# Pairing the tiles of the plain layer norms: one logarithm and one exponential for two tiles' variances, and six banks for centered tiles

## The reference

```python
def _layernorm(x, axis=-1, eps=1e-05):
    m = jnp.mean(x, axis=axis, keepdims=True)
    v = jnp.var(x, axis=axis, keepdims=True)
    return (x - m) / jnp.sqrt(v + eps)

def _ln(x, g, b, eps=1e-05):
    mu = jnp.mean(x, axis=-1, keepdims=True)
    var = jnp.var(x, axis=-1, keepdims=True)
    return (x - mu) * jax.lax.rsqrt(var + eps) * g + b
```

## Time and profile before

| | us |
|---|---|
| runs | 3423.56, 3425.92, 3431.12; median 3425.92 |
| the profiled execution: its own time | 3423.85 |
| its span, first to last instruction | 3422.1 |
| busy: PE, DVE, ACT, POOL | 3107.2, 2148.8, 1799.2, 1170.2 |
| one norm of the gamma kind, from its first matmul to its last DVE operation | 20.5 |

### The profile page before, as it was taken

The page is one execution under the profiler, slowest core; times in us unless marked ns, Lnnn a source line. Parts: engine busy times, 40 slices in busy tenths (PEclk is TensorE's granted clock), DMA queues, the critical chain, the costliest instruction groups (busy, mean ns, idle before and its releaser), DMA issues. The chain is left out here.

```text
span 3422.1 us, 62042 instructions
## 1 busy us (share of the span) xinstructions
PE 3107.2 (91%) x22950; PEld 1935.5 (57%) x22971; DVE 2148.8 (63%) x4177; ACT 1799.2 (53%) x3979; POOL 1170.2 (34%) x1166
## 2 busy tenths in 40 slices
PE   7999989999999999998898879997699999998999
PEld 6999866446464646446654543334366566664444
DVE  7999744025353545337847744445699999974777
ACT  1232245564746474755644433334466666664666
POOL 4666511001010101105626612224477777760000
PEclk9999989999999999999999989998899999999999
DMA  2000000000000000000000022220100000003676
GB/s 86 20 15 10 1 19 12 1 7 1 6 1 6 1 6 4 3 7 1 1 8 1 1 64 56 57 51 16 24 11 5 4 5 4 5 1 45 72 68 65
DMA packets 75395, 66.43 MB, mean 19 GB/s; under 512 B 20374, under 2 KB 70584, under 8 KB 74680
## 3 DMA queue, kind: packets, MB, share of 16 engines
q1 hardware_dynamic: 75096, 62.45, 10.7%
HBM read 55.58 MB, written 2.51 MB: 17 GB/s over the span
## 5 line engine op out<-in xcount | busy, mean ns | idle before, releaser
L707 ACT ACTIVATE p_hidden<-p_hid_ps,net_bias 128x344 f32<-128x344 f32 x816 | 381.9, 548 | 229.2 <-PE p_hid_ps L654 170.0
L2447 POOL TENSOR_TENSOR p_qt<-p_qt,p_q_sum 97x512 f32<-97x512 f32 (+1 forms) x44 | 46.3, 1053 | 734.2 <-DVE p_q_sum L2401 734.2
L680 PE MATMUL p_y_ps<-p_hidden,net_down 128*64 128x344 f32 x1632 | 284.6, 468 | 4.2 <-DVE p_hidden L756 4.1
L654 PE MATMUL p_hid_ps<-xn,net_up 64*128 64x344 f32 x1248 | 241.6, 488 | 8.2 <-PEq L316 4.6
L2759 DVE TENSOR_TENSOR p_hid<-p_silu,p_pair_ps 128x344 f32<-128x344 f32 x288 | 134.8, 509 | 173.1 <-PE p_pair_ps L2708 95.1
L756 DVE TENSOR_TENSOR p_hidden<-p_hidden,p_row 128x344 f32<-128x344 f32 x384 | 175.6, 515 | 74.4 <-ACT p_hidden L707 47.0
L2740 ACT ACTIVATE p_silu<-p_pair_ps 128x344 f32<-128x344 f32 x288 | 116.0, 455 | 201.6 <-PE p_pair_ps L2697 201.6
L1919 POOL TENSOR_TENSOR p_rot<-p_rot,p_cross 128x512 f32<-128x512 f32 x128 | 160.4, 1274 | 127.3 <-DVE p_cross L2074 127.3
L680 PEld LDWEIGHTS p_y_ps<-p_hidden,net_down 128*64 128x64 f32 x1632 | 102.8, 136 | 158.9 <-issue 49.2
L1932 POOL TENSOR_TENSOR p_prob<-p_prob,p_total 128x1024 f32<-128x1024 f32 (+1 forms) x128 | 185.4, 1469 | 13.1 <-DVE p_total L2100 13.1
L654 PEld LDWEIGHTS p_hid_ps<-xn,net_up 64*128 64x128 f32 x1248 | 105.9, 189 | 129.0 <-ACT p_hidden L707 78.7
(11 more groups left out here) (465 smaller groups left out, 8102.6 us busy)
## 6 DMA issues: line engine op xcount, KB each, us to landing
p_row<-gated_rows SPq DMA_DIRECT2D x192, 86.0 KB, 2.9
p_row<-mark_rows SPq DMA_DIRECT2D x192, 86.0 KB, 10.3
tok_x<-in_tok_x SPq DMA_DIRECT2D x11, 384.0 KB, 3.1
out<-h SPq DMA_DIRECT2D x12, 172.0 KB, 3.7
shared_value_pairs<-shared_values SPq DMA_DIRECT2D x16, 128.0 KB, 2.5
p_swapped<-xn SPq DMA_DIRECT2D x64, 32.0 KB, 1.9
p_x<-in_tok_x SPq DMA_DIRECT2D x5, 384.0 KB, 3.1
p_kinds<-in_tok_c3w SPq DMA_DIRECT2D x1, 1280.0 KB, 7.2
```

The costliest lines, as they stand in the source:

```text
L654: mm = pe.matmul(hid_ps[k % ring][:, 0:TILE], w_up[half(g), n, :], x[half(g), cols(t)], start=True, stop=not experts or by_rows)
L680: mm = pe.matmul(y_ps[u][half(g), 0:TILE], w_down[:, n, :], hid[k % hidden_ring][:], start=n == 0, stop=last and not experts)
L707: act.activation(hid[k % hidden_ring][:], hid_ps[k % ring][:, 0:TILE], func, bias=b_up[:, n:n + 1]).then_inc(act_done.sem, 1)
```

## The change

Tiles are taken in pairs. `var_ps` becomes one tensor of two banks, with an even tile's variances in the first and an odd tile's in the second; `both` is a view of 2 x 344 columns over them. One logarithm and one exponential of 688 columns (`roots(n)`) take the place of two each of 344. The four banks of `var_ps` become two, and the four of `centered_ps` six. `square` has four buffers, `rstd` three of two tiles each. `variance(t)` of an even tile now waits until the logarithm of the pair before has read the two banks, and stands two places behind `spread` in PE's order in place of one. ACT does the two squares of a pair, then logarithm and exponential of the pair before. DVE's order stays, with each `scale` waiting for its pair's exponential.

```diff
-    nc, banks, ring = tower.nc, 4, 3
+    nc, banks, ring, turns = tower.nc, 6, 4, TILES // 2
...
-        var_ps = [ph.ps(f"var{r}") for r in range(banks)]
+        var_ps = ph.ps("var", (P, 2 * BANK))
         square = [ph.sb(f"square{r}", [P, TILE]) for r in range(ring)]
-        rstd = [ph.sb(f"rstd{r}", [P, TILE]) for r in range(ring)]
+        rstd = [ph.sb(f"rstd{r}", [P, 2, TILE]) for r in range(3)]
+        both = var_ps[:].rearrange("p (i c) -> p i c", c=BANK)[:, :, 0:TILE]
...
                     pe.wait_ge(squared.sem, squared.at(t + 1))
-                    if t >= banks:
-                        pe.wait_ge(logged.sem, logged.at(t - banks + 1))
-                    pe.matmul(var_ps[t % banks][:, 0:TILE], tower.average[:], square[t % ring][:],
+                    if t >= 2 and t % 2 == 0:
+                        pe.wait_ge(logged.sem, logged.at(t // 2))
+                    pe.matmul(both[:, t % 2, :], tower.average[:], square[t % ring][:],
                               start=True, stop=True).then_inc(var_ready.sem, 1)
-                for s in range(TILES + 1):
+                for s in range(TILES + 2):
                     if center and s < TILES:
                         spread(s)
-                    if s >= 1:
-                        variance(s - 1)
+                    if s >= 2:
+                        variance(s - 2)
...
+                def roots(n):
+                    act.wait_ge(var_ready.sem, var_ready.at(2 * n + 2))
+                    if n >= 3:
+                        act.wait_ge(scaled.sem, scaled.at(2 * (n - 2)))
+                    act.activation(rstd[n % 3][:], both, ACT.Ln, bias=tower.eps[eps]).then_inc(logged.sem, 1)
+                    act.wait_ge(logged.sem, logged.at(n + 1))
+                    act.activation(rstd[n % 3][:], rstd[n % 3][:], ACT.Exp, scale=-0.5).then_inc(rooted.sem, 1)
+
+                for n in range(turns + 1):
+                    if n < turns:
+                        squares(2 * n)
+                        squares(2 * n + 1)
+                    if n >= 1:
+                        roots(n - 1)
...
-                    dve.wait_ge(rooted.sem, rooted.at(t + 1))
+                    dve.wait_ge(rooted.sem, rooted.at(t // 2 + 1))
```

More of the change, by code:

```diff
@@ L116, in norm_phase @@
 def norm_phase(tower, src, dst, eps, center=True, gamma=None, beta=None, clip=None, residual=False, pos=None, loads=(), then=None):
-    nc, banks, ring = tower.nc, 4, 3
+    nc, banks, ring, turns = tower.nc, 6, 4, TILES // 2
     with phase(tower) as ph:
         centered_ps = [ph.ps(f"centered{r}") for r in range(banks)]
-        var_ps = [ph.ps(f"var{r}") for r in range(banks)]
+        var_ps = ph.ps("var", (P, 2 * BANK))
         square = [ph.sb(f"square{r}", [P, TILE]) for r in range(ring)]
-        rstd = [ph.sb(f"rstd{r}", [P, TILE]) for r in range(ring)]
+        rstd = [ph.sb(f"rstd{r}", [P, 2, TILE]) for r in range(3)]
+        both = var_ps[:].rearrange("p (i c) -> p i c", c=BANK)[:, :, 0:TILE]
         centered = ph.counts(TILES if center else 0)
-        squared, var_ready, logged, rooted, scaled = [ph.counts(TILES) for _ in range(5)]
+        squared, var_ready, scaled = [ph.counts(TILES) for _ in range(3)]
+        logged, rooted = ph.counts(turns), ph.counts(turns)
         loaded = ph.counts(16 * len(loads))
@@ L198, in scale @@
                 def scale(t):
-                    dve.wait_ge(rooted.sem, rooted.at(t + 1))
+                    dve.wait_ge(rooted.sem, rooted.at(t // 2 + 1))
                     if gamma is None:
-                        ins = dve.tensor_tensor(dst[:, cols(t)], values(t), rstd[t % ring][:], ALU.mult)
+                        ins = dve.tensor_tensor(dst[:, cols(t)], values(t), rstd[t // 2 % 3][:, t % 2, :], ALU.mult)
                     else:
-                        ins = dve.scalar_tensor_tensor(dst[:, cols(t)], values(t), gamma, rstd[t % ring][:],
+                        ins = dve.scalar_tensor_tensor(dst[:, cols(t)], values(t), gamma, rstd[t // 2 % 3][:, t % 2, :],
                                                        ALU.mult, ALU.mult)
```

## The result

| | before | changed |
|---|---|---|
| median of 5 runs, us | 3425.73 (3423.56 to 3431.12) | 3441.69 (3437.97 to 3445.26) |
| profiled execution / span, us | 3423.85 / 3422.1 | 3437.97 / 3436.2 |
| ratio changed / before | | 1.0045, 95% interval 1.003 to 1.006 |
| a gamma norm at full clock, us | 20.54 | 21.77 |
| busy ACT, us | 1799.2 | 1778.2 |

The change made the kernel 16.0 us slower (3441.69 - 3425.73). ACT did 21.0 us less work and nothing came of it.

What follows compares the result with a forecast made beforehand. Neither PE nor ACT was full; waits around four centered banks bound each norm. The new waits added +12.1 us over 15 norms, giving 3436.0 from the profiled execution and 3438.0 from the median; middle 3437, range 3427 to 3448.

Steps and rivals of the forecast that it cites:

- The ring: In each norm, logarithm end to logarithm end: hand-over 0.05, variance matmul 0.68, spread 0.58, second variance 0.77, logarithm 0.82; 2.90 us a pair.
- the tail: End of a gamma norm after the last exponential: five DVE operations, 2.04 us, against 1.23 before.
- The exposed weight load: A matmul that had to wait loads its weights in the open: next matmul 0.68 us later, against 0.58 in a stream.
- the hand-over from ACT to PE: From a logarithm's end to the start of the variance matmul waiting for it: 0.05 us, an estimate.
- the kinds: Norm calls by type: gamma 8 (+6.6 us), two-tensor 3 (+3.3), one-step 2 (+1.2), clip 1 (+0.9), uncentered 1 (-0.7).
- the sum: All 15 norms together: 6.6 + 3.3 + 1.2 + 0.9 - 0.7 + 0.8 = +12.1 us.
- cold starts: Two norm calls that begin at half clock, with one more matmul before their first logarithm: 0.4 us each, +0.8.
- The uncentered norm: The one call without spreads: 2.32 us between logarithms, 15.8 us against 16.5 before, -0.7.
- one of the two things that by the forecast would show it wrong: Forecast wrong if logarithms stood under 2.75 us apart, or if the uncentered call weren't the only one to become shorter.
- The third rival: TensorE idle 1.4 us after a norm's dummy matmuls, against 0.92, drops the clock at half the norms: +17, 3454; chance 0.09.
- The first rival: Reordering lets weight loads run ahead, so 0.58 replaces 0.68: 9 us less over all norms, 3429; chance 0.15.
- The second: Rival: waiting for the logarithm isn't last; PE's matmuls (2.32) or ACT's work (up to 2.50) pace a pair: 3410; chance 0.06.

Runs made afterwards that it cites:

- the kernel with PE's order in pairs: Changed kernel with TensorE doing both spreads of a pair, then both variances of the pair before: 3448.14 us, ratio 1.0066 to before; gamma norm 19.88 us.

## Why the prediction was right, and where it was off

The forecast was 3437 (range 3427 to 3448), slower, with 0.77. The time is 3441.69.

The ring was right in its members and its place, and the kernel with PE's order in pairs shows that it sets the pace. Forecast 2.90 us, measured 2.99. The logarithm of 688 columns was put at 0.82 and took 0.83, the exponential 0.78 and 0.78, the first logarithm came 3.75 us after the first matmul (forecast 3.77), the tail took 2.02 (forecast 2.04). The exposed weight load is there: 0.14 to hand over and 0.66 to the next matmul, 0.80 together, where the forecast had 0.05 + 0.68 = 0.73. The mis-sized term is the hand-over from ACT to PE: 0.14 us, where the forecast had 0.05, an estimate whose only row was a hand-over from ACT to DVE. Here the logarithm's wait is an instruction of its own ahead of the weight load. The other members cancel to within 0.01, so each of five rings is 0.09 us longer and the last exponential ends 0.44 us later than forecast (19.76 for 19.32), and a gamma norm is 0.41 us longer: 21.77 for 21.36. Over the kinds this makes +17.7 at full clock where the sum had 11.3 without its cold starts.

The uncentered norm was forecast 0.7 us shorter. At full clock it is (16.8 for 17.0, less than thought for the same hand-over), but in this kernel it ran at 1.2 GHz for 17.1 us and took 6.3 us more than before. That is one of the two things that by the forecast would show it wrong, and it did come: the uncentered call became longer. The reason was the clock, which the forecast priced for other places only. The third rival looked for the clock's fall in the longer idle time after the dummy matmuls; it fell instead inside that norm and at the start of two gamma norms. Its price was 10.4 us gross, less the 2.6 of a cold start that went. So the norms together are 25.5 us longer in the trace, where the sum had 12.1. The other stages gave 11.4 us back, which the forecast did not have and which is the clock's doing at least in part. That the total came out only 4.7 us over the forecast is in part luck: two errors of opposite sign. The sign of the change isn't, since the code at full clock alone adds 17.7.

The first rival (no exposed load, 3429) falls: the ring was longer, not shorter. The second (ACT's saved work sets the pace) is wrong for this order of PE's instructions, and came close to true with the other order, where the spacing is 2.4 to 2.6. The rule from "Perfetto Trace Analysis", section "Optimizing Scalar/DVE Operations" in the Trainium skill, that larger operations help where the engine is saturated, agrees with what the traces show: full pairs lost where ACT waited for PE in every pair (0.42 us at each second square), and where ACT had no gap a paired exponential took a pair from 2.60 to 2.38 us.

## What to carry to other kernels

Before two instructions are merged, draw the ring that their shared buffer closes: with one double buffer, everything between the reader's end and the next reader's start is paid in series, and the merged work's saved fixed cost lies beside it. Look at what order the producer works in, since one foreign matmul between two that are waited for cost about 0.47 us a pair here. Read the granted clock of each stage after every change of schedule: a wait of 3.6 us on TensorE ahead of a stage was worth 31 us in one kernel and 4 to 6 in another.

## What the runs showed of the hardware

- A logarithm from PSUM over two banks, 2 x 344 columns in rows 512 apart, took 0.833 us on the mean of 90, 0.295 more than one of 344 columns: 0.86 ns for each further column. The exponential of 688 columns, SBUF to SBUF, took 0.287 more than one of 344, so reading a second bank costs 0.01 us at most by these rows.
- Of two waits ahead of a matmul, the order mattered: with the late one written last the matmul started 0.14 us after the release, with the late one first 0.06. The one that is written last is an instruction of its own, 51 ns long; the other is carried by the weight load.
- A granted clock of 0.50 held for 82 us under a TensorE that was 99% busy, in a stage that other kernels ran at 1.00, or in which the clock came back after 10 us at half.
- In the norms the low stretches of the clock repeated at the same operations in two executions of one program, to the same length (17.1 and 3.4 us); elsewhere some did not. Other kernels had them at other places, even where the instructions up to there were the same (a gamma norm at 0.87 in one, at 1.00 in the other).
- Stages with the same code took 255.4 us with 3.4 us at half clock in them, 258.5 to 259.7 with 13.7, and 262.3 to 262.6 with 20.5 to 23.9.
